# Node numbers as places, 109 edge rows, and strided copies made from DRAM in a two-layer graph kernel

## The reference, cut to what matters

```python
def _gin_conv(x, src, dst, n, W1, b1, gamma, beta, W2, b2):
    agg = jax.ops.segment_sum(x[src], dst, num_segments=n)
    h = x + agg
    h = jax.nn.relu(_batchnorm(h @ W1 + b1, gamma, beta))
    return jax.nn.relu(h @ W2 + b2)
```

## Time and profile before

| what | value |
|---|---|
| runs shown | 2775.24 us median, 2773.72 to 2776.81, 3 runs |
| profiled execution | 2784.43 us, of which the span is 2782.6 us |
| mean granted TensorE clock | 0.94 |
| indirect DMAs on POOL | 224 raw, 1648 of the lists (96 x 8 in layer 1, 110 x 8 in layer 2) |
| strided copies | 217 DMAs in each layer |

### The profile page before, as it was taken

The page is one execution under the profiler, slowest core; times in us unless marked ns, Lnnn a source line. Parts: engine busy times, 40 slices in busy tenths (PEclk is TensorE's granted clock), DMA queues, the critical chain, the costliest instruction groups (busy, mean ns, idle before and its releaser), DMA issues.

```text
span 2782.6 us, 30723 instructions
## 1 busy us (share of the span) xinstructions
PE 2371.1 (85%) x10215; PEld 1827.6 (66%) x10215; DVE 1739.1 (62%) x3502; ACT 551.3 (20%) x1605; POOL 1815.2 (65%) x1894
## 2 busy tenths in 40 slices
PE   1466777999999999999979566699999999988979
PEld 1134433878877777777758444588888888776767
DVE  7999997755555555555548577555555555544459
ACT  8975544300000000000009311000000000000038
POOL 2058777777777777777740477677777777777720
PEclk8687766999999999999989899999999999999999
DMA  9387998888888888888848999888888888888868
GB/s 309 141 261 224 285 306 254 250 260 251 253 253 255 254 255 254 254 254 254 254 153 279 328 334 325 285 283 286 287 284 284 287 285 282 260 254 253 253 203 270
DMA packets 309364, 734.28 MB, mean 264 GB/s; under 512 B 41510, under 2 KB 183730, under 8 KB 309198
## 3 DMA queue, kind: packets, MB, share of 16 engines
q0 software_dynamic: 149184, 550.97, 63.2%
q1 hardware_dynamic: 160014, 181.25, 20.8%
HBM read 579.47 MB, written 152.59 MB: 263 GB/s over the span
## 4 chain that ended last, share of the span: by engine, by line
PE 51%; DMA 23%; POOL 8%; SPq 8%; ACT 5%; issue 4%; DVE 1%; DVEq 0%; ACTq 0%; POOLq 0%
PE agg_ps L830 35%; DMA rows<-node_rows,src_all 17%; SPq L617 7%; PE sort_ps L955 6%; PE sort_ps L872 5%; POOL rows L697 5%; DMA rows<-node_rows,raw_list 4%; PE sort_ps L876 2%; DMA raw_more<-node_rows,raw_list 2%; PE agg_ps L779 2%; ACT acc L1001 2%; POOL raw_more L679 2%; ACT lane_code L988 1%; ACT lane_code L977 1%; POOL rows L679 1%
## 5 line engine op out<-in xcount | busy, mean ns | idle before, releaser
L697 POOL DMA_INDIRECT rows<-node_rows,src_all x1648 | 1558.2, 946 | 642.6 <-issue 346.4
L830 PE MATMUL agg_ps<-rows,work 128*128 128x256 f32 (+1 forms) x7004 | 1630.3, 387 | 188.9 <-DMA rows<-node_rows,src_all 140.8
L830 PEld LDWEIGHTS agg_ps<-rows,work 128*128 128x128 f32 x7004 | 1297.7, 191 | 494.3 <-issue 133.9
L1582 DVE SCALAR_TENSOR_TENSOR acc<-agg_ps,in_first,acc 128x256 f32 (+1 forms) x286 | 138.7, 485 | 944.1 <-PE agg_ps L830 856.7
L1032 ACT ACTIVATE bn_root<-bn_var 128x2 f32<-128x2 f32 x3 | 0.6, 203 | 1860.2 <-DVE bn_var L1168 1860.2
L679 POOL DMA_INDIRECT rows<-node_rows,raw_list x124 | 129.2, 1042 | 174.8 <-DMA node_rows<-acc 137.3
L1534 DVE TENSOR_TENSOR work<-lane_code,lane_ps 128x1024 f32<-128x1024 f32 (+1 forms) x206 | 228.1, 1107 | 1.0 <-issue 1.0
L955 PE MATMUL sort_ps<-early,work 128*128 128x256 f32 x784 | 175.3, 388 | 22.1 <-ACT work L1117 11.5
L955 PEld LDWEIGHTS sort_ps<-early,work 128*128 128x128 f32 x784 | 140.2, 194 | 57.5 <-issue 25.6
L1543 DVE TENSOR_TENSOR work<-lane_code,lane_ps 128x640 f32<-128x640 f32 x206 | 167.7, 814 | 0.0
L1117 ACT ACTIVATE work<-acc,bn_shift,bn_scale 128x128 f32<-128x128 f32 x392 | 166.5, 485 | 3.3 <-DVE bn_shift L1179 2.8
(11 more groups left out here) (246 smaller groups left out, 1844.8 us busy)
## 6 DMA issues: line engine op xcount, KB each, us to landing
node_rows<-acc SPq DMA_DIRECT2D x113, 260.0 KB, 6.3
rows<-node_rows,src_all POOLq DMA_INDIRECT x1648, 4.4
node_rows<-acc SPq DMA_DIRECT2D x27, 910.0 KB, 4.3
node_rows<-acc SPq DMA_DIRECT2D x57, 390.0 KB, 5.4
node_rows<-acc SPq DMA_DIRECT2D x28, 650.0 KB, 8.6
node_rows<-acc SPq DMA_DIRECT2D x114, 130.0 KB, 4.6
acc<-in_x SPq DMA_DIRECT2D x13, 896.0 KB, 11.0
rows<-in_x SPq DMA_DIRECT2D x13, 896.0 KB, 7.3
```

The lines of the kernel that those rows point to most:

```text
L697: pool.indirect_dma_start(tile_rows(k, 0, ROWS_OF[t] * DP), None, tables[layer][0:NPOS if t >= LAST_STRIDED else TABLE, :], bass.IndirectO ...
L830: mm = pe.matmul(bank[:, 0:width], hot[:, unit * P:(unit + 1) * P], tile_rows(k, row, width), start=(start and n == 0), stop=(stop and n = ...
L1582: dve.scalar_tensor_tensor(to, sums, lanes[:, g:g + 1], to, ALU.mult, ALU.add).then_inc(sums_added, 1)
```

## The change: node numbers as places, copies from DRAM to DRAM

A place is now the node's number: `places` maps block `b`, partition `p` to row `b * 128 + p`, and there are 12600 places. A store of seven blocks writes 896 pieces of 1040 bytes. LR becomes 1950, so that there are 109 edge rows and 95 x 8 + 109 x 8 list tiles. The strided copies read the natural part of the table in DRAM and write another part of it: for a group of 14 blocks and a stride s there are s DMAs, 133 in a layer (50224 rows of 1040 bytes), each spread over 16 equal parts. Before each, SP waits until the natural rows of its group have landed. In layer 1 they are still paced by the raw tiles; in layer 2 all of them are issued after the last natural rows, none beside the dense stage. TWICE becomes 108: the natural tiles of all rows but the last are gathered before POOL waits for the copies. `add_self` waits for the natural rows alone. VectorE's setup has two instructions fewer.

```diff
-PITCH = NB + 7
-NPOS = P * PITCH
+NPOS = 12600
-LR = 1932
+LR = 1950
-TWICE = 80
+TWICE = NR - NR % 2
...
         def places(table, b0, b1):
-            return table[0:NPOS, :].rearrange("(p b) f -> p b f", b=PITCH)[:, b0:b1, :]
+            return table[b0 * P:b1 * P, :].rearrange("(b p) f -> p b f", p=P)
...
+        def copied_to(stride, i):
+            return (i * GROUP * P if i < GROUPS else NPOS) // (16 * stride) * (16 * stride)
+        def copies_of_group(table, i):
+            for stride in STRIDES:
+                first, end = copied_to(stride, i), copied_to(stride, i + 1)
+                n = (end - first) // (16 * stride)
+                for place in range(first, first + stride):
+                    yield (places_of(table, place_in(stride, place), [(n, 16), (1, n)]),
+                           places_of(table, place, [(n * stride, 16), (stride, n)]), 16 * n)
...
-            for n, (to, of) in enumerate(copies):
+            sp.wait_ge(spare_stored, 2 * SPARE)
+            for n, (i, to, of) in enumerate(copies):
+                sp.wait_ge(rows_stored[i], ROWS_STORED[0][i])
                 beside_tile = n * COPIES_UNTIL // len(copies)
...
             for c in range(NCH - 1):
                 store_rows(1, c, y_out, (c + 1) * CH)
-                rows_beside = 0
-                while c % 2 + c // 2 and rows_beside < BESIDE:
-                    i, to, of = next(copies)
-                    sp.dma_start(to, of).then_inc(group_stored[i], 16)
-                    rows_beside += of.shape[0] * of.shape[1]
             store_last_rows()
-            for i, to, of in copies:
-                sp.dma_start(to, of).then_inc(group_stored[i], 16)
+            while issued < len(copies):
+                copy_next()
...
-                act.wait_ge(table_stored, TABLE_DMAS[layer])
-                if layer == 0:
-                    act.wait_ge(copies_stored, COPIES)
                 for b in range(NB):
-                    if layer and b % GROUP == 0:
-                        act.wait_ge(group_stored[b // GROUP], GROUP_COPIES)
+                    if b % GROUP == 0:
+                        act.wait_ge(rows_stored[b // GROUP], ROWS_STORED[layer][b // GROUP])
...
-            setup(dve.tensor_scalar(key_ints[:, 0:GIVEN], src_int, P - 1, None, ALU.bitwise_and))
-            setup(dve.tensor_scalar(src_places, src_int, 7, None, ALU.logical_shift_right))
+            setup(dve.tensor_scalar(key_ints[:, 0:LR], dst_int[:, 0:LR], P - 1, None, ALU.bitwise_and))
+            setup(dve.tensor_copy(src_rows, src_int))
             setup(dve.tensor_tensor(self_edges, src_int[:, 0:LR], dst_int[:, 0:LR], ALU.is_equal))
-            setup(dve.scalar_tensor_tensor(src_rows, key_ints[:, 0:GIVEN], float(PITCH), src_places, ALU.mult, ALU.add))
-            setup(dve.tensor_scalar(key_ints[:, 0:LR], dst_int[:, 0:LR], P - 1, None, ALU.bitwise_and))
```

More of the change, by code:

```diff
@@ L215 @@
 assert PAIRS_BESIDE * RAW_GROUPS >= NPAIR and RAW % RAW_GROUP == 0 and 0 < LAST_EDGES <= P and 4 * SORT + RAW_INSIDE * DP <= RING * DP
-assert SRC_CAP > NPOS + UP and all(NPOS % s == 0 and i + 1 == min(s, 6) - 2 for i, s in enumerate(STRIDES))
+assert PAD_SRC + UP >= SRC_CAP > NPOS + UP and NPOS > NPAD and all(NPOS % s == 0 and i + 1 == min(s, 6) - 2 for i, s in enumerate(STRIDES))
 assert NB * (QUARTER + 1) <= RING * DP and 4 * SORT <= RING * DP and X_SLOTS * CH * D <= RING * DP
@@ L388, in build @@
         group_stored = [sem(f"group_stored{i}") for i in range(GROUPS)]
-        table_stored = sem("table_stored")
+        rows_stored = [sem(f"rows_stored{i}") for i in range(GROUPS)]
         copies_stored = sem("copies_stored")
@@ L490, in places_of @@
             return bass.AP(table.tensor, table.offset + first_row * DP, [[step * DP, n] for step, n in steps] + [[1, DP]])
[L492 to L502, removed]
-            for stride in STRIDES:
-                yield from strided_places(table, stride, b0, b1, lambda first, n, step: block_rows(first, first + (n - 1) * step + 1, step))
-        zeros = early[:, 0:RAWS * DP].rearrange("p (b f) -> p b f", f=DP)
+        def copied_to(stride, i):
+            return (i * GROUP * P if i < GROUPS else NPOS) // (16 * stride) * (16 * stride)
+        def copies_of_group(table, i):
+            for stride in STRIDES:
+                first, end = copied_to(stride, i), copied_to(stride, i + 1)
[3 more added lines that the diff above has]
+                           places_of(table, place, [(n * stride, 16), (stride, n)]), 16 * n)
+        zeros = early[:, 0:DP]
         def spare_places(table):
-            yield places(table, NB, PITCH), zeros[:, 0:PITCH - NB]
+            yield table[NPAD:NPOS, :], zeros[0:NPOS - NPAD]
             for stride in STRIDES:
-                yield from strided_places(table, stride, NB, PITCH, lambda first, n, step: zeros[:, 0:n])
-            yield table[TABLE - 8:TABLE, :], zeros[0:8, 0]
+                first = copied_to(stride, GROUPS)
+                for place in range(first, first + stride):
+                    n = len(range(place, NPOS, stride))
+                    if n:
+                        yield table[place_in(stride, place):place_in(stride, place) + n, :], zeros[0:n]
+            yield table[TABLE - 8:TABLE, :], zeros[0:8]
         EDGE_PIECES = ((0, 96), (96, NR - 1 - 96), (NR - 1, 1))
@@ L564, in store_rows @@
                 b0, b1 = c * CH, (c + 1) * CH
[L565 to L570, removed]
+                sp.dma_start(places(tables[t], b0, b1), block_rows(b0, b1)).then_inc(rows_stored[c // 2], 16)
             def store_last_rows():
@@ L593, in _ @@
                              allow_slow_non_contiguous=True).then_inc(consts_loaded, 16)
-            copies = [(to, of) for i in range(GROUPS) for to, of in copies_of_blocks(tables[0], i * GROUP, (i + 1) * GROUP)]
-            for n, (to, of) in enumerate(copies):
+            copies = [(i, to, of) for i in range(GROUPS) for to, of, _ in copies_of_group(tables[0], i)]
+            sp.wait_ge(spare_stored, 2 * SPARE)
+            for n, (i, to, of) in enumerate(copies):
+                sp.wait_ge(rows_stored[i], ROWS_STORED[0][i])
                 beside_tile = n * COPIES_UNTIL // len(copies)
@@ L672, in _ @@
             pool.wait_ge(spare_stored, 2 * SPARE)
-            pool.wait_ge(table_stored, TABLE_DMAS[0])
+            for i in range(GROUPS):
+                pool.wait_ge(rows_stored[i], ROWS_STORED[0][i])
             for g in range(RAWS):
@@ L702, in _ @@
             for layer in range(2):
-                pool.wait_ge(table_stored, TABLE_DMAS[layer])
+                for i in range(GROUPS):
+                    pool.wait_ge(rows_stored[i], ROWS_STORED[layer][i])
                 if layer:
```

36 lines of the change are left out of this document (19 added, 17 removed).

## The result

The kernel after takes **2792.81 us** (median of 4 runs, 2790.68 to 2796.36), the kernel before on the same chip 2774.48 (4 runs): ratio 1.0063, 95% interval 1.0049 to 1.0077, some 18 us slower. The forecast was 2882, so the sign was right and the size was not: +18 in place of +107. The profiled execution took 2793.49 us with a span of 2791.7.

A forecast was written before the change was run, and what follows sets the result against it. POOL's gathers and its waits between them were taken as the bound, copies as much in two stretches. Layer 1 +45 - 10, layer 2 -10 - 5 - 11.7 + 99 made +107 on 2775.2, 2882 us; 8-in-10 range 2755 to 2985.

The forecast's parts named there:

- the price of the copies, taken as 1.5 passes: DRAM-to-DRAM copies: middle between write cost alone (171 and 158 us) and read plus write; 256 us layer 1, 237 layer 2.
- two passes: Rival: the copies' read and write add up in full on the DMA engines; +271 us, 3046 us; chance 0.13.
- neither end has a nearer row: Copy price: no profile row favours either bound, one reason for taking the middle, 1.5 passes.
- the one-pass rival: Rival: DMA engines take a row from DRAM as from SBUF; -17 us, 2758 us; chance 0.20.
- Layer 1, +45: Raw tiles: copies need 45 us beyond the 211 left, so POOL's first list gather waits.
- Layer 2, +87: Stop ahead of layer 2's list: POOL waits 99 us for copies in place of 11.7.
- One row less, -10 and -10: One edge row less: eight gathers fewer in each layer at 1.25 us, -10 us in each.
- The dense stage, -5: Layer 1's dense stage: SP's queue empty of copies, last pieces land sooner, POOL starts about 5 us earlier.
- Setup, natural rows in short pieces, ScalarE's waits, TensorE's 4%: Smaller parts: VectorE's setup, 1040-byte natural pieces (0 to +3 each), ScalarE's dropped waits, TensorE's spare time; all taken as 0.
- about even: Rival: copies at 1.05 to 1.25 passes, pause 28 to 60 us, time some -8 to +25 us; chance 0.09.
- point of decision, 1.1 passes: POOL's wait after the natural tiles: copy price, about 300 GB/s, where the longer pause eats all of the gains.

The follow-up runs named there:

- after_again: The changed kernel, unaltered, profiled again on one chip with the kernel before: 2803.05 us, where the kernel before took 2782.36.
- rows_110_again: The changed kernel with 110 edge rows (of 1932) instead of 109, run a second time: median 2823.40 us, ratio 1.0184 to the kernel before.
- copies_alone_sbuf: The kernel before with natural tiles of 2 rows first and no copies beside the dense stage, so its copies from SBUF run alone: 2946.26 us.
- rows_110: The changed kernel with 110 edge rows (of 1932) instead of 109, first single run: 2835.72 us.

## Why the prediction was right or wrong

**What bounds the kernel** was read rightly. The gathers of POOL at 1.25 us and what POOL waits for between them set the end in every run here, and each experiment moved the time by what it moved in those.

**The failed step is the price of the copies, taken as 1.5 passes.** Put into the prediction's own sum, a stop of 42.5 us means copies of 42.5 + 146 - 8 = 180 us, 1.14 passes of 158, and the 49.66 of after_again 1.19. The queues of 1540 to 1855 say the same without that sum: 183 us, 1.16 passes.

Part of this is the size of the pass. The sum took the joint rate of 331 GB/s for the copies, but the earlier trace rows has their own price beside gathers, 298 GB/s, by which a pass is 175 us and one pass alone makes a stop of 37. Of such passes the copies from DRAM took 1.05, and beside the raw tiles a byte of them cost 1.01 times one out of SBUF (the queues of 300 to 440). So in company the new source adds next to nothing, and alone it costs 1.19 times the old one.

The reason given for two passes, that a mix goes no faster than either alone, did not carry: the mix of gathers and copies was compared with a stretch of stores in long pieces, while copies in pieces of 1040 bytes run at 284 GB/s by themselves. The right reading of the 331 GB/s would have been that a mix goes faster than its slower part. A measured price of copies alone would not have mended the forecast: 218 us in its sum give a stop of 80. And with "neither end has a nearer row" the middle was only a choice; the one-pass rival said that an engine may be limited by its pieces and not by where they lie, and long pieces from DRAM at 319 GB/s speak for it.

**Layer 1, +45** became +2.1, with no wait. At 1.14 passes the copies need 195 us, and 211 were left, so by the prediction's own working there was room (up to 1.24). The term fell with the price, not with its formula.

**Layer 2, +87** became +41.8 on one chip and a stop of 42.5 on the other. The formula held: 183 and 136 us of the engines, 319, filled the 315 us of the stretch. What it left out is small: the gathers beside the copies became dearer (136 us in place of 130), and the last part, where copies run alone, is slower (248 GB/s) than the mean price.

**One row less, -10 and -10:** -8.9 and -8.0 in the two walks. As an edit by itself the row is worth more (rows_110_again, 18.4 us in the stretch that the copies end), which the sum had at 0 and whose reason stays open.

**The dense stage, -5:** -9.2. With SP's queue empty POOL began 3.7 us after the last issue, as the 4.3 us of landing said; taking the copies out of before's dense stage alone (copies_alone_sbuf) made the idle time 118.26 us, where the earlier trace rows has 127.06. So this gain comes from the removal and not from the new places.

**Setup, natural rows in short pieces, ScalarE's waits, TensorE's 4%:** +1.1 ahead of the first raw gather, and nothing in the walks; TensorE is at 96% in the walk of layer 2 (767.80 of 800 us), as before, and POOL's longest wait for it is 0.9 us.

**The rivals.** What happened is "about even", which had 0.09: it gave stops of 28 to 60 us and some -8 to +25 us for 1.05 to 1.25 passes. Its share was too small because the prices were spread evenly between two far ends. The one-pass rival's point of decision, 1.1 passes, is borne out as far as it goes: at 1.14 to 1.19 the change is slower, by 0.6%. The rival's mechanism, engines limited by pieces and not by where they lie, came nearest to what the queues show beside other transfers; its 20 us of stop came from the pass of 158. (At 1.8 passes the sum gives 2982 and not 2985; nothing hangs on it.)

**The agreement that was none.** The middle of the bounds lay close to the 244 us that follow from the 214 GB/s of the Trainium skill (page "DMA: Bandwidth & Descriptors", section "Latency and other measured facts"). The copies of layer 2 took 180 us by the sum, so two numbers near each other, one a chosen middle and the other for other pieces, supported nothing.

## What to carry to other kernels

Where a change moves transfers from beside one stage to behind it, first ask what the stage leaves idle: here the DMA engines stood at 0.44 in the dense stage while the same copies made POOL wait 42 us later, and putting a part of them back was worth more than the change had cost. Copies from DRAM to DRAM cost almost what copies out of SBUF cost beside other transfers here, and more alone (239 against 284 GB/s). So where no row shows the transfer, look for rows of the same piece length in the same company, and take each queue's own share and not the joint rate, before splitting the difference between far ends. Copies beside a stage should stop some time before the stage's last store, since that store is what the next stage waits for.

## What the runs showed of the hardware that was not expected

- Copies in pieces of 1040 bytes, nothing beside them: 284 GB/s from SBUF to DRAM, 239 from DRAM to DRAM; in packets of 11.9 KB from DRAM to DRAM 319.
- Two queues (SP's and ScalarE's) moved 240 GB/s together where SP's alone moved 239.
- The same copies ran beside gathers at a joint 296 (rows_110) to 315 GB/s, and when the gathers stopped the engines, still full (1.05 to 1.07), moved only 237 to 248.
- The kernel before took 2771.97 and 2774.48 us in two series (medians) and 2784.77 to 2785.12 on the other chips, a difference more than half as large as the effect that was to be measured.
